# Gated attention and expert layer: the attention stage's order around the maximum, and an expert stage in which GpSimd only fetches

## The chip, the cores and the metric

The kernel runs on one core of a Trainium2 chip. A core has TensorE (PE in the profile, its weight loads PEld), VectorE (DVE), ScalarE (ACT), GpSimd (POOL) and SyncE (SP), which work through their own instruction lists and wait for each other on semaphores, and 16 DMA engines. The metric is the device time of one execution in microseconds, the median of the runs.

## The reference

128 sequences of 128 tokens and 256 channels in float32 pass through a windowed attention over a context, and then through a layer with 16 experts of which each token takes two:

```
x = x + tanh(g_xattn) * attention(layernorm(x), ctx, ctx)      # 16 heads of 16, rope, |i-j| <= 64, softmax, output projection
x = x + tanh(g_ffn) * experts(layernorm(x))
def experts(x):                          # per sequence
    probs, ei = top_k(softmax(x @ w_router), 2)
    buf[ei, pos] = x                     # 16 places for each expert and sequence, the rest is dropped
    o = (silu(buf @ w_gate) * (buf @ w_fc)) @ w_proj
    return sum(probs * o[ei, pos])
```

## The kernel before

There are three blocks, one behind the other: attention, routing, experts. Products in float32 precision are made of three passes over operands split in a head (rounded to the matmul's format) and a rest; ScalarE makes the heads ("_hi"), VectorE or GpSimd the rests ("_lo").

**Attention.** A step treats a pair of sequences; there are 64. Each engine has its list of the step's parts written out by hand (its `step(s)`), in which parts of several pairs are interleaved: at step s the scores, maxima, exponentials and values are those of pair s, the projections of keys and queries those of pair s + 1, the transposes of the input those of s + 2, the output projection that of s - 1, the second norm and the router those of s - 2. The two sequences of a pair are its halves b = 0 and b = 1. For each half TensorE writes scores in the four banks ST0 to ST3 (L680, with the band mask L685); VectorE takes partial maxima (`partial_max`, L506, one of each bank); TensorE turns them (`turn_max`, L693); VectorE makes the shift (`shift_of`, L513 and L517); TensorE subtracts it in the banks (`subtract_max`, L700); ScalarE takes the exponentials (`exp_unit`, L360); TensorE multiplies with the values (`values_unit` 0 to 3, L712, one for each bank) into the bank PO, which ScalarE copies out (`copy_out_t`). Then TensorE transposes back (`untranspose`, L724), VectorE divides (`normalise`: the reciprocal L525, the product L527), TensorE transposes the attention output (`attention_t`, L730), and ScalarE and VectorE split it (`attention_head`, at_hi, L401; `attention_rest`, at_lo, L565) for the output projection. L730 is also the line of the transposes of the input (`inputs_t`) and of the second norm (`normed2_t`). VectorE's `scale` makes q_cos and q_sin, from which GpSimd makes q_rot, and ScalarE q_head.

**Experts.** A step treats one unit, 128 in all: one sequence in the parts that move tokens, one pair of experts over a group of 8 sequences in the parts that multiply. The constants LOAD, PICK, DISPATCH, GATE, HIDDEN, OUTPUT, FETCH, COLLECT (L1047) say by how many steps a part lags: a part with lag -11 treats unit u + 11 at step u. SyncE loads a sequence's normed tokens (scaled<-xn_d), ScalarE rounds them (x_hi), GpSimd takes the rest (x_lo, L1163), VectorE builds the 0/1 matrix `pick` (L1219), TensorE gathers with it into DS (L1304), ScalarE and VectorE split the result (s_hi, s_lo). For a pair of experts TensorE multiplies (GU, L1260 to L1262), ScalarE takes tanh of half the gate (th, L1196), VectorE makes (th + 1) * gate (L1236) and the product with the other half (hid, L1240), TensorE transposes (HT) and multiplies (EO); the result goes to memory (eo_d). GpSimd fetches each token's two rows from there with two indirect DMAs (L1154, `first` and `second`), SyncE fetches the attention's result (scaled<-x_d), and VectorE adds them, weighted (L1229, L1244), which SyncE writes out. The names th, hid and scaled are tiles in SBUF; `scaled` here holds the tiles of loaded and finished tokens. The halving in silu(g) = g (1 + tanh(g / 2)) / 2 lies in `weight` (L984).

## Time and profile before

| | |
|---|---|
| median of 3 runs | 1761.66 us (1759.19 to 1764.53) |
| the profiled execution's own time | 1754.3 us |
| its span, first to last instruction | 1752.5 us |
| mean granted TensorE clock | 0.96 |
| busy over the span | PE 1481.3, DVE 1408.6, ACT 1146.4, POOL 1086.1 us |
| attention stage | about 0 to 1200 us |
| routing | about 1200 to 1264 us |
| expert stage | about 1264 to 1752 us |

The table's times are of one execution. Busy time adds up an engine's instructions; an instruction's recorded time can overlap the next one's by 0.1 us or so, so the distance between starts says what an instruction costs its engine.

### The profile page before, as it was taken

Reading aid. Unit: us, or ns where it says so; the run is one execution under the profiler, and the core shown is the slowest. Engines: PE = TensorE matmul, PEld = TensorE weight load, DVE = VectorE, ACT = ScalarE, POOL = GpSimd, SP = SyncE. Lnnn points to the kernel's source line nnn. Section 1 sums busy time; section 2 is a strip of 40 time slices with the busy share of each in tenths; the row PEclk is TensorE's granted clock in tenths of the full one; section 3 lists DMA queues with packets and bytes.
Section 4 is the critical chain, followed back from the end, with each engine's and each line's share of the span. In section 5 each row is a group of like instructions: output and inputs, shape, how many; then the busy total and the mean of one; then the engine's idle time right before and its main releaser. Section 6 shows DMA issues by size and latency. Waiting matters only on the chain. (4 is left out here: it accounts for less than half of the span.)

```text
span 1752.5 us, 50746 instructions
## 1 busy us (share of the span) xinstructions
PE 1481.3 (85%) x16844; PEld 1195.2 (68%) x16844; DVE 1408.6 (80%) x2993; ACT 1146.4 (65%) x2321; POOL 1086.1 (62%) x1490
## 2 busy tenths in 40 slices
PE   3899999999999999999999999982199888888881
PEld 3676667777776676777676677761088888888881
DVE  3788888888888888878888888867878999999984
ACT  3777777777777777777777777764065555555550
POOL 3555656565655656565565656534638887888876
PEclk9999999999999999999999999995589999999995
DMA  3122121212222121212212121430037888888887
GB/s 94 50 76 75 61 89 60 90 60 84 65 67 82 60 90 60 90 60 78 71 62 88 60 90 60 137 119 30 15 106 245 260 261 258 261 273 263 264 261 223
DMA packets 156096, 210.21 MB, mean 120 GB/s; under 512 B 18688, under 2 KB 104832, under 8 KB 156032
## 3 DMA queue, kind: packets, MB, share of 16 engines
q1 hardware_dynamic: 125312, 142.36, 25.9%
q0 software_dynamic: 12288, 33.57, 6.7%
q10 hardware_dynamic: 18432, 33.56, 5.3%
q8 instruction: 24, 0.39, 0.1%
q14 instruction: 40, 0.33, 0.1%
HBM read 125.54 MB, written 83.89 MB: 119 GB/s over the span
## 5 line engine op out<-in xcount | busy, mean ns | idle before, releaser
L506 DVE TRANSPOSE_TENSOR_REDUCE part_max<-ST 128x16 f32<-128x512 f32 x512 | 321.3, 685 | 136.6 <-PE ST L685 136.6
L360 ACT ACTIVATE probs_t<-ST 128x512 f32<-128x512 f32 x512 | 264.4, 604 | 27.6 <-PE ST L700 27.4
L712 PE MATMUL PO<-probs_t,v_aug 128*32 128x128 f32 x4096 | 193.6, 284 | 67.9 <-ACT probs_t L360 55.4
L299 POOL TENSOR_TENSOR k_rot<-k_cos,k_sin 128x256 f32<-128x256 f32 x64 | 47.1, 736 | 268.5 <-DVE k_sin L544 268.5
L712 PEld LDWEIGHTS PO<-probs_t,v_aug 128*32 128x32 f32 x4096 | 88.9, 109 | 161.1 <-ACT probs_t L360 154.0
L1191 ACT ACTIVATE x_hi<-scaled 128x256 fp32r<-128x256 f32 x128 | 53.5, 418 | 214.8 <-DMA scaled<-xn_d 168.5
L401 ACT ACTIVATE at_hi<-F 128x512 fp32r<-128x512 f32 x64 | 38.2, 597 | 187.8 <-PE F L730 187.8
L1260 PE MATMUL GU<-we_hi,s_hi 128*128 128x256 f32 x512 | 155.4, 304 | 0.2 <-DVE s_lo L1250 0.2
L1154 POOL DMA_INDIRECT second<-eo_d,collect_row x128 | 123.0, 961 | 42.2 <-issue 28.6
L1163 POOL TENSOR_TENSOR x_lo<-scaled,x_hi 128x256 fp32r<-128x256 f32 x128 | 118.4, 925 | 49.3 <-ACT x_hi L1191 47.3
L1154 POOL DMA_INDIRECT first<-eo_d,collect_row x128 | 124.4, 972 | 37.3 <-issue 20.6
L1261 PE MATMUL GU<-we_hi,s_lo 128*128 128x256 f32 x512 | 144.9, 283 | 0.0
L1262 PE MATMUL GU<-we_lo,s_hi 128*128 128x256 f32 x512 | 144.8, 283 | 0.0
L316 POOL TENSOR_TENSOR q_rest<-q_rot,q_head 128x512 f32<-128x512 f32 x64 | 82.2, 1284 | 78.7 <-ACT q_head L413 78.7
L1260 PE MATMUL EO<-we_hi,h_hi 128*128 128x256 f32 x256 | 81.6, 319 | 50.3 <-issue 43.5
L730 PE MATMUL F<-ident_sb,xn 128*128 128x128 f32 x512 | 86.2, 292 | 31.1 <-ACT xn L437 19.7
L366 ACT ACTIVATE out_t<-PO 128x512 f32<-128x512 f32 x128 | 76.7, 599 | 53.2 <-PE PO L712 53.2
L1229 DVE SCALAR_TENSOR_TENSOR scaled<-first,weight,scaled 128x256 f32<-128x256 f32 x128 | 65.5, 512 | 49.6 <-issue 18.1
L1261 PEld LDWEIGHTS GU<-we_hi,s_lo 128*128 128x128 f32 x512 | 98.3, 192 | 0.0
L1260 PEld LDWEIGHTS GU<-we_hi,s_hi 128*128 128x128 f32 x512 | 97.6, 191 | 0.4 <-issue 0.4
L1262 PEld LDWEIGHTS GU<-we_lo,s_hi 128*128 128x128 f32 x512 | 97.8, 191 | 0.0
L1260 PEld LDWEIGHTS EO<-we_hi,h_hi 128*128 128x128 f32 x256 | 48.3, 188 | 70.0 <-issue 68.1
(158 smaller groups left out, 5610.7 us busy)
## 6 DMA issues: line engine op xcount, KB each, us to landing
eo_d<-eo ACTq DMA_DIRECT2D x128, 256.0 KB
x_in_sb<-x SPq DMA_DIRECT2D x64, 256.0 KB, 2.8
c_in_sb<-ctx_t SPq DMA_DIRECT2D x64, 256.0 KB, 2.9
xr_sb<-x SPq DMA_DIRECT2D x64, 256.0 KB, 4.0
x_d<-x SPq DMA_DIRECT2D x64, 256.0 KB, 4.0
xn_d<-xn SPq DMA_DIRECT2D x64, 256.0 KB, 4.2
scaled<-xn_d SPq DMA_DIRECT2D x128, 128.0 KB, 4.0
scaled<-x_d SPq DMA_DIRECT2D x128, 128.0 KB
```

The source lines that it names most:

```text
L316: pool.tensor_tensor(q_rest[:].rearrange("p k t -> p (k t)"), q_rot[:].rearrange("p k t -> p (k t)"), q_head[:].rearrange("p k t -> p (k t ...
L360: act.activation(probs_t[:, b, i].rearrange("p j q -> p (j q)"), ST[i][:], ACT.Exp) \
L366: act.activation(out_t[:, b].rearrange("p i q -> p (i q)"), PO[:], ACT.Copy).then_inc(M["ot_copied"], 1)
L506: dve.tensor_reduce(part_max[:, i, 0], ST[i][:].rearrange("p (c l) -> p c l", l=32), AX_X, ALU.max, apply_transpose=True).then_inc(M["part ...
L712: last = pe.matmul(PO[32 * j:32 * j + 32, i * SEQ:(i + 1) * SEQ], v_aug[:, n.par, b, head], probs_t[:, b, i, j], start=True, stop=True)
L730: last = pe.transpose(F[:, (2 * k + b) * SEQ:(2 * k + b + 1) * SEQ], src[:, b, k * P:(k + 1) * P], ident[:])
L1154: pool.indirect_dma_start(out=dst[:, n.turn(3)], out_offset=None, in_=D["eo_d"][n.group].rearrange("r e c -> (r e) c"), in_offset=bass.Ind ...
L1163: pool.tensor_tensor(x_lo[:, n.slot(2)], x_in_sb[:, n.turn(3)], x_hi[:, n.slot(2)].bitcast(F32), ALU.subtract).then_inc(M["x_lo_done"], 1)
L1229: dve.scalar_tensor_tensor(out=y_sb[:, n.slot(2)], in0=first[:, n.turn(3)], scalar=weight[:, 0, bass.ds(n.n, 1)], in1=xr[:, n.turn(3)], op ...
L1260: pe.matmul(out, lh, rh, start=first, stop=False)
L1261: pe.matmul(out, ll, rh, start=False, stop=False)
L1262: return pe.matmul(out, lh, rl, start=False, stop=last)
```

## The change

In the attention stage TensorE turns the maximum of half 0 behind three of the query projection's twelve matmuls, not six, and that of half 1 ahead of both output projections, not between them; it subtracts the shift ahead of the transposes of the attention output, not behind; the transposes of the second norm stand behind values unit 2, not ahead of it. VectorE takes the product of `normalise` behind the shift (the reciprocal stays ahead), and one of the two statistics of the norm behind the shift of half 1. ScalarE takes exponentials 0 and 1 of half 0 ahead of at_hi, and ct_hi (`context_head`) behind the exponentials of half 1.

In the expert stage x_lo is made by VectorE; GpSimd only fetches. ScalarE takes Silu in place of tanh, and VectorE's operation (th + 1) * gate is gone, with the factor 0.5 in `weight`. Rings and lags change: four tiles for loads and four for the attention's result, in which the output is now added up in place, a HEAD part of its own for x_hi, loads 14 steps ahead instead of 13, fetch and collect one step later. The lists of SyncE, ScalarE and VectorE are in another order.

```diff
@@ ACT, attention, step @@
                 normed2(s - 2)
+            if s.real:
+                exp_unit(s, 0, 0)
+                exp_unit(s, 0, 1)
             if (s - 1).real:
                 attention_head(s - 1)
             if s.real:
-                for i in range(4):
-                    exp_unit(s, 0, i)
+                exp_unit(s, 0, 2)
+                exp_unit(s, 0, 3)
                 copy_out_t(s, 0)
...
-            if (s + 2).real:
-                context_head(s + 2)
             if s.real:
                 for i in range(4):
                     exp_unit(s, 1, i)
             if (s + 2).real:
+                context_head(s + 2)
                 input_head(s + 2)
@@ DVE, attention @@
+        def reciprocals(n, b):
+            dve.wait_ge(M["o2_done"], n.n * 2 + b + 1)
+            wait_for(dve, M["att_done"], n.n * 2 + b - 1)
+            o2 = F2[:].rearrange("p (h d) -> p h d", d=32)
+            dve.reciprocal(rden[:, b], o2[:, :, DK]).then_inc(M["rden_done"], 1)
...
             if (s - 1).real:
+                reciprocals(s - 1, 1)
+            if s.real:
+                shift_of(s, 0)
+            if (s - 1).real:
                 normalise(s - 1, 1)
-            if s.real:
-                shift_of(s, 0)
...
             if s.real:
                 shift_of(s, 1)
+            if (s + 3).real:
+                norm_rest(s + 3)
@@ PE, attention, step @@
                 key_projection(s + 1)
-                query_projection(s + 1, 0)
+                query_projection(s + 1, 0, [0])
             if s.real:
                 turn_max(s, 0)
             if (s + 1).real:
+                query_projection(s + 1, 0, [1])
                 query_projection(s + 1, 1)
+            if s.real:
+                subtract_max(s, 0)
             if (s - 1).real:
                 attention_t(s - 1)
             if s.real:
-                subtract_max(s, 0)
                 values_unit(s, 0, 0)
                 values_unit(s, 0, 1)
+                values_unit(s, 0, 2)
             if (s - 2).real:
                 normed2_t(s - 2)
             if s.real:
-                values_unit(s, 0, 2)
                 values_unit(s, 0, 3)
                 scores(s, 1)
...
+            if s.real:
+                turn_max(s, 1)
             if (s - 1).real:
                 output_projection(s - 1, 0)
-            if s.real:
-                turn_max(s, 1)
-            if (s - 1).real:
                 output_projection(s - 1, 1)
@@ experts @@
-    LOAD, PICK, DISPATCH, GATE, HIDDEN, OUTPUT, FETCH, COLLECT = -13, -11, -9, 0, 2, 3, 12, 14
+    LOAD, HEAD, PICK, DISPATCH, GATE, HIDDEN, OUTPUT, FETCH, COLLECT = -14, -11, -10, -9, 0, 2, 3, 13, 15
...
-            n = unit(PICK)
-            if on(PICK):
-                pool.wait_ge(M["x_hi_done"], n.n + 1)
-                wait_for(pool, M["ds_done"], n.n - 1)
-                pool.tensor_tensor(x_lo[:, n.slot(2)], x_in_sb[:, n.turn(3)], x_hi[:, n.slot(2)].bitcast(F32),
-                                   ALU.subtract).then_inc(M["x_lo_done"], 1)
...
-                act.activation(th[:, n.slot(2)], GU[n.slot(2)][:].rearrange("p (e f n) -> p e f n", e=2, f=2)[:, :, 0],
-                               ACT.Tanh, scale=0.5).then_inc(M["th_done"], 1)
+                wait_for(act, M["ht_done"], n.n - 1)
+                act.activation(gate[:, n.slot(2)], GU[n.slot(2)][:].rearrange("p (e f n) -> p e f n", e=2, f=2)[:, :, 0],
+                               ACT.Silu).then_inc(M["gate_done"], 1)
```

TensorE's list near the end of the attention stage, where it is written out step by step; the rows begin with the last matmul of the query projection (F<-xt_lo,w_hi) of a half 0 and end with its last values unit. Before:

```order
L668 MATMUL F<-xt_lo,w_hi 128x256
L730 MATMUL F<-ident_sb,att 128x128 x4
L700 MATMUL ST<-shift,ones_r 128x512 x4
L712 MATMUL PO<-probs_t,v_aug 32x128 x8
L730 MATMUL F<-ident_sb,xn 128x128 x4
L712 MATMUL PO<-probs_t,v_aug 32x128 x8
```

and of the change:

```order
L680 MATMUL F<-xt_lo,w_hi 128x256
L712 MATMUL ST<-shift,ones_r 128x512 x4
L742 MATMUL F<-ident_sb,att 128x128 x4
L724 MATMUL PO<-probs_t,v_aug 32x128 x12
L742 MATMUL F<-ident_sb,xn 128x128 x4
L724 MATMUL PO<-probs_t,v_aug 32x128 x4
```

The subtraction has moved ahead of the attention transposes, and one values unit (four matmuls) ahead of the transposes of the second norm.

ScalarE's list at the same place, from the second norm to the copy of the transposed second norm. Before:

```order
L445 ACTIVATE xn<-x,off,rstd 128x256 x2
L401 ACTIVATE at_hi<-F 128x512
L360 ACTIVATE probs_t<-ST 128x512 x4
L366 ACTIVATE out_t<-PO 128x512
L384 ACTIVATE x2t<-F 128x512
```

and of the change:

```order
L445 ACTIVATE xn<-x,off,rstd 128x256 x2
L360 ACTIVATE probs_t<-ST 128x512 x2
L401 ACTIVATE at_hi<-F 128x512
L360 ACTIVATE probs_t<-ST 128x512 x2
L366 ACTIVATE out_t<-PO 128x512
L384 ACTIVATE x2t<-F 128x512
```

at_hi has moved between the second and the third exponential.

VectorE's list of one expert step in the middle of the stage. Before:

```order
L1214 TENSOR_TENSOR h_lo<-HT,h_hi 128x256
L1219 TENSOR_TENSOR pick<-logits,iota_sb 128x256
L1229 SCALAR_TENSOR_TENSOR scaled<-first,weight,scaled 128x256
L1236 SCALAR_TENSOR_TENSOR th<-th,GU 128x256
L1240 TENSOR_TENSOR hid<-th,GU 128x256
L1244 SCALAR_TENSOR_TENSOR scaled<-second,weight,scaled 128x256
L1250 TENSOR_TENSOR s_lo<-DS,s_hi 128x32x16
```

and of the change:

```order
L1220 TENSOR_TENSOR h_lo<-HT,h_hi 128x256
L1226 TENSOR_TENSOR x_lo<-scaled,x_hi 128x256
L1228 TENSOR_TENSOR pick<-logits,iota_sb 128x256
L1237 TENSOR_TENSOR gate<-gate,GU 128x256
L1242 SCALAR_TENSOR_TENSOR scaled<-first,weight,scaled 128x256
L1248 TENSOR_TENSOR s_lo<-DS,s_hi 128x32x16
L1253 SCALAR_TENSOR_TENSOR scaled<-second,weight,scaled 128x256
```

x_lo has come in, the operation on th is gone, and both weightings stand behind the gate's product, the second one last.

## Rows read from the trace of the kernel before

**Rows 1.** Timeline of PE, one attention pair: start us, us, engine, line, operation.

```profile
611.32 0.39 PE L680 MATMUL ST<-q_hi,k_hi 32*128 32x256 f32 x4 [0.19 <-issue]
...
615.40 0.27 PE L693 MATMUL PO<-ident_sb,part_max 128*128 128x128 f32 x1
...
616.79 0.51 PE L700 MATMUL ST<-shift,ones_r 32*128 32x512 f32 x4
618.07 0.92 PE L712 MATMUL PO<-probs_t,v_aug 128*32 128x128 f32 x16 [0.77 <-ACT probs_t L360]
618.92 0.66 PE L730 MATMUL F<-ident_sb,xn 128*128 128x128 f32 x4
619.50 0.64 PE L712 MATMUL PO<-probs_t,v_aug 128*32 128x128 f32 x16
620.08 0.39 PE L680 MATMUL ST<-q_hi,k_hi 32*128 32x256 f32 x4
...
624.49 0.27 PE L693 MATMUL PO<-ident_sb,part_max 128*128 128x128 f32 x1
...
625.88 0.51 PE L700 MATMUL ST<-shift,ones_r 32*128 32x512 f32 x4 [0.21 <-DVE shift L517]
...
629.15 0.39 PE L680 MATMUL ST<-q_hi,k_hi 32*128 32x256 f32 x4
```

**Rows 2.** Busy us and counts of two stretches, granted clock, DMA share, GB/s.

```profile
1290.00:1310.00 20.00, 20.00 (x168) 19.85 (x167) 14.80 (x34) 12.77 (x33) 4.43 (x6) 1.00 0.40 135
...
1330.00:1690.00 360.00, 317.06 (x2477) 299.23 (x2477) 333.27 (x722) 203.59 (x514) 297.04 (x309) 1.00 0.85 263
```

**Rows 3.** Groups of DVE from 1330 to 1690 us: busy, mean ns.

```profile
L1244 DVE SCALAR_TENSOR_TENSOR scaled<-second,weight,scaled 128x256 f32<-128x256 f32 x103 | 77.6, 753 | 0.0
```

**Rows 4.** Timeline of DVE, expert steps, the last row from the tail.

```profile
1453.08 0.48 DVE L1244 SCALAR_TENSOR_TENSOR scaled<-second,weight,scaled 128x256 f32<-128x256 f32 x1
...
1457.49 0.41 DVE L1214 TENSOR_TENSOR h_lo<-HT,h_hi 128x256 fp32r<-128x256 f32 x1
1457.83 0.41 DVE L1219 TENSOR_TENSOR pick<-logits,iota_sb 128x256 fp32r<-128x256 f32 x1
...
1458.55 0.41 DVE L1236 SCALAR_TENSOR_TENSOR th<-th,GU 128x256 f32<-128x256 f32 x1
...
1459.33 1.06 DVE L1244 SCALAR_TENSOR_TENSOR scaled<-second,weight,scaled 128x256 f32<-128x256 f32 x1
...
1460.91 0.41 DVE L1214 TENSOR_TENSOR h_lo<-HT,h_hi 128x256 fp32r<-128x256 f32 x1
...
1732.53 0.48 DVE L1244 SCALAR_TENSOR_TENSOR scaled<-second,weight,scaled 128x256 f32<-128x256 f32 x1
```

**Rows 5.** Timeline of DVE, the same attention pair.

```profile
612.57 2.51 DVE L506 TRANSPOSE_TENSOR_REDUCE part_max<-ST 128x16 f32<-128x512 f32 x4 [0.59 <-PE ST L685]
...
615.71 0.30 DVE L513 TENSOR_REDUCE PO<-PO 128x32 f32<-128x128 f32 x1
616.05 0.69 DVE L517 TENSOR_TENSOR shift<-PO,own_sb 128x512 fp32r<-128x512 f32 x1
...
621.32 2.51 DVE L506 TRANSPOSE_TENSOR_REDUCE part_max<-ST 128x16 f32<-128x512 f32 x4 [1.60 <-PE ST L685]
```

**Rows 6.** Timeline of ACT, the same attention pair.

```profile
616.86 0.60 ACT L401 ACTIVATE at_hi<-F 128x512 fp32r<-128x512 f32 x1 [3.09 <-PE F L730]
617.42 2.07 ACT L360 ACTIVATE probs_t<-ST 128x512 f32<-128x512 f32 x4
```

**Rows 7.** Timeline of POOL, the same expert step.

```profile
1459.98 1.00 POOL L1163 TENSOR_TENSOR x_lo<-scaled,x_hi 128x256 fp32r<-128x256 f32 x1
```

**Rows 8.** Timeline of POOL, the tail of the expert stage.

```profile
1732.03 0.94 POOL L1154 DMA_INDIRECT first<-eo_d,collect_row  x1 [0.30 <-issue]
```

**Rows 9.** Loads of xn_d from 1400 to 1600 us, issue to landing.

```profile
DMA to landing us min/median/max: 2.9/4.1/5.2
```

**Rows 10.** Timeline of ACT, start of the kernel.

```profile
0.74 1.28 ACT L351 ACT_TABLE_LOAD   x1 [0.74 <-PEq L1377]
```

More of the change, by code:

```diff
@@ L552, in norm_stats, with norm_rest @@
             wait_for(dve, M["ln_aggr"], n.n)
-            for b in range(2):
-                last = dve.bn_stats(stats[:, b], x_in_sb[:, n.par, b])
-            last.then_inc(M["ln_stats"], 1)
+            dve.bn_stats(stats[:, 0], x_in_sb[:, n.par, 0])
+        def norm_rest(n):
+            dve.bn_stats(stats[:, 1], x_in_sb[:, n.par, 1]).then_inc(M["ln_stats"], 1)
             dve.wait_ge(M["ln_stats"], (n + 1).n)
@@ L732, in transposes, with project @@
             return last
-        def project(F, w, hi, lo, m):
-            for k in range(KC):
+        def project(F, w, hi, lo, m, parts=range(KC)):
+            for k in parts:
                 last = split_matmul(F[:, m * 2 * SEQ:(m + 1) * 2 * SEQ],
@@ L771, in logits_t, with query_projection @@
             pe.transpose(F2[:, 256:320], lt_sb[:], ident[0:64, 0:64]).then_inc(M["lg_done"], 1)
-        def query_projection(n, m):
-            if m == 0:
+        def query_projection(n, m, parts=range(KC)):
+            if m == 0 and 0 in parts:
                 pe.wait_ge(M["xt_hi_done"], (n + 1).n)
                 pe.wait_ge(M["xt_lo_done"], (n + 1).n)
-            last = project(F0, 0, xt_hi, xt_lo, m)
+            last = project(F0, 0, xt_hi, xt_lo, m, parts)
             if m == KC - 1:
@@ L1183, in step @@
             if on(OUTPUT):
+                act.wait_ge(M["eo_done"], n.n + 1)
+                wait_for(act, eo_out[n.turn(3)], (n - 3).landed(3))
+                act.activation(flat(eo[:, n.turn(3)]), EO[n.slot(2)][:], ACT.Copy).then_inc(M["eo_copied"], 1)
+            n = unit(OUTPUT)
+            if on(OUTPUT):
                 act.wait_ge(M["eo_copied"], n.n + 1)
@@ L1251, in step @@
                                   tokens(s_hi, n).bitcast(F32), ALU.subtract).then_inc(M["s_lo_done"], 1)
+            n = unit(COLLECT)
+            if on(COLLECT):
+                dve.wait_ge(M["y_part_done"], n.n + 1)
+                dve.scalar_tensor_tensor(out=xr[:, n.turn(4)], in0=second[:, n.turn(3)],
+                                         scalar=weight[:, 1, bass.ds(n.n, 1)], in1=xr[:, n.turn(4)],
+                                         op0=ALU.mult, op1=ALU.add).then_inc(M["out_done"], 1)
         run_flat(dve, step)
```

107 lines of the change are left out of this document (46 added, 61 removed).

## The prediction, on record before the change ran

> **What bounds the kernel now.** I read the work of each engine by stretches first, then the timelines of one attention pair and of one expert step. The attention stage takes 64 pairs; from one pair's first scores to the next pair's is 629.15 - 611.32 = 17.83 us [rows 1]. TensorE sets it: its instructions follow each other with hardly a gap, and where it does wait, it waits for the exponentials (0.77 us at 618.07). I call the stretch from scores of half 0 to scores of half 1 "half 0" (620.08 - 611.32 = 8.76 us), the rest "half 1" (9.07 us). The expert stage is another matter. In its middle, 360 us hold 103 steps, 3.49 us each [rows 2, 3]; VectorE is busy 333 us of them, TensorE 317, and the DMA engines 0.85 of the time [rows 2]. In one undisturbed step VectorE runs without a gap from h_lo at 1457.49 to h_lo at 1460.91, 3.42 us [rows 4]: VectorE sets the step. The mean is 0.07 us more because some steps are held up by late transfers.
>
> **Attention, half 0.** The last of the four partial maxima ends at 612.57 + 2.51 = 615.08 [rows 5], while TensorE reaches the turn of the maximum only at 615.40 [rows 1], behind the whole first half of the query projection (six matmuls, 0.12 us apart, as 24 fill 2.86 us further on). After the change three matmuls of 0.12 us come behind the turn instead of ahead of it, so TensorE is there at about 615.05 and waits for the maxima: 615.08, 0.06 for the signal (shift ends at 616.74 and the subtraction starts at 616.79 [rows 1, 5]), 0.1 for the weight load, so the turn runs at 615.24. VectorE's own sequence from there is as before: the reduction started 0.31 after the turn and the shift ended 1.03 after the reduction started (615.71 to 616.74 [rows 5]); the attention product, now behind the shift, is out of the way. So the shift ends at 615.24 + 0.31 + 1.03 = 616.58 and the subtraction starts at 616.64 instead of 616.79, 0.15 us earlier. The first exponential starts 0.63 after it (616.79 to 617.42 [rows 1, 6]), at 617.27.
>
> ScalarE is where it is given back. Before, at_hi (the rounded copy of the transposed attention output) ran at 616.86 and was done at the moment when the first exponential could start, so it cost nothing [rows 6]. Now the order is exponential 0, 1, at_hi, exponential 2, 3. Exponentials are 0.49 apart ((2.07 - 0.60)/3, with at_hi's 0.60 as one's length), at_hi delays what is behind it by 617.42 - 616.86 = 0.56 [rows 6]. Exponential 2 so starts at 617.27 + 0.98 + 0.56 = 618.81 and its values can run 0.65 later (617.42 to 618.07), at 619.46. TensorE reaches that place at 617.27 + 0.49 + 0.65 + 0.29 = 618.70 and has nothing else to do there, since the transposes of the second norm (0.58: 618.92 to 619.50 [rows 1]), which filled this wait, now stand behind values unit 2. From 619.46: values 2 (0.29, half of 619.50 to 620.08), transposes 0.58, values 3 0.29; the scores of half 1 start at 620.62 instead of 620.08. Half 0 gets **0.54 us longer**. (The attention transposes do move into the wait for exponential 0, but a wait takes their place between values 1 and 2.)
>
> **Attention, half 1.** The maxima of half 1 are ready at 621.32 + 2.51 = 623.83 [rows 5], and the turn ran at 624.49 between the two output projections [rows 1]. Put ahead of both, it runs at 623.99 (signal and weight load as above), where TensorE is free since about 623.7 (624.49 less six matmuls): a wait of 0.2 to 0.35. The shift is then early and the wait for it, 0.21 us at 625.88 [rows 1], goes; but the projections start later by the wait. I count 0.12 us gained, between 0 and 0.2. What else moves is covered: at_lo, q_cos and q_sin are late by about 0.55 beyond the longer half 0's beginning and meet slack on ScalarE, because ct_hi, which now stands behind the four exponentials, has left 0.6 us ahead of them. xt_hi then ends some 0.3 us later and xt_lo still just ahead of the next maxima. Behind a late at_hi stand, in order, at_lo on VectorE, q_sin, q_rot on GpSimd, q_head; if their slack were gone, half 1 would grow too.
>
> Sum of the attention stage: +0.42 us a pair, 62 pairs with all their parts: **+26 us**; bounds 0.2 a pair (12 us) and 0.6 (37 us).
>
> **Expert stage, VectorE.** An undisturbed step is 3.42 us. The multiplication with (th + 1) goes (0.41 [rows 4], 0.44 with its share of a gap); x_lo comes from GpSimd and costs what pick does, 0.34 a step. The second weighting (L1244) takes 1.06 in this step and 0.48 in the one at 1453.08; over the stretch its mean is 0.753 [rows 3, 4]. What stretches it is GpSimd's x_lo: it starts at 1459.98 [rows 7], and the weighting ends 0.41 behind that, at 1460.39, wherever it began; both take two operands from SBUF. A fetch doesn't do this: in the tail, where no x_lo is left, the weighting at 1732.53 runs inside the fetch of 1732.03 and takes 0.48 [rows 4, 8]. With x_lo gone from GpSimd, 0.58 us of this step goes. 3.42 - 0.44 - 0.58 + 0.34 = 2.74 us.
>
> The Trainium skill ("SBUF — State Buffer", section "SBUF: two separate sides") describes an exclusive lock between a GpSimd operation and a VectorE operation with two SBUF inputs, and speaks against the change if a fetch counts as such an operation, since GpSimd now does nothing else and VectorE has four such operations a step. By it the 0.58 would come back at least once a step; the weighting in the tail shows no such thing.
>
> **What bounds the step then.** TensorE: before the weightings began, 168 matmuls and transposes of 24 a step filled 20 us, 2.86 us a step [rows 2]. GpSimd: two fetches, 2 x (0.95 + 0.30) = 2.5 us [rows 8]. DMA: 0.85 x 3.49 = 2.97 us of all engines a step, at 263 GB/s [rows 2], and the bytes stay the same. So the transfers become the nearest bound, and a FIFO of three queues isn't kept full: with transfers landing in 4.1 us (2.9 to 5.2) at 0.85 busy [rows 9], gathered rows and x1 have only some 5 to 6 us between their issue and the first weighting two steps later. I take 0.96 busy, 3.10 us a step; the ends are 2.97 and 3.35 (0.89 busy, near what they do now). Gain 0.39 us x 101 steps = **40 us**, ends 52 and 14. The earlier loads (four input tiles, an SP queue that no longer waits for the weighting) are what lets the transfers come that near.
>
> Smaller terms: the fetch is one step later, so the tail, in which only fetches run, has one more step: +2.5 us [rows 8]. Silu brings one more table load, 1.28 us like the one at the start [rows 10], nothing hides it wholly: +1.3. In the first ten dispatches x_lo of 0.7 us on GpSimd is out of the chain: -2. Silu itself and the rest of the routing cost nothing.
>
> Sum: +26 - 40 + 2.5 + 1.3 - 2 = -12 us. The profiled run took 1754.3 us (span 1752.5), 7.4 less than the median of the runs, 1761.7; I put the difference on the median: **1749 us**.
>
> **Rivals.**
> 1. The attention edits don't lose (at_hi fits, or TensorE's waits were worth more than I read): the stage stays or gains a little. For it: TensorE's waits for exponentials are the only real ones there. Against: ScalarE has no room between exponentials 1 and 2, by its own row. 1749 - 26 = 1723. Chance 0.18.
> 2. Slower: the expert step is held by transfers at 3.35 us, because a fetched row or x1 lands too late for the in-order VectorE, and the tiles' ring stops the loads: 1749 + 26 = 1775; it decides from 3.23 us a step on. For it: steps are held up already at 0.85 busy (mean 3.49 against 3.42). Against: each load is issued earlier relative to its user. Chance 0.16.
> 3. The attention stage loses 0.8 us a pair, since the chain at_lo, q_sin, q_rot, q_head has no slack after all: 1749 + 24 = 1773. Chance 0.06.
> 4. Fetches stretch VectorE as x_lo did: 2.74 + 0.58 = 3.32 us a step, 1749 + 22 = 1771. The row in the tail is against it. Chance 0.02.
> My forecast, attention slower by 12 to 37 and the expert stage faster by 30 to 50, has 0.53; 0.05 is left for what I don't see.
>
> **How the numbers follow.** A run can tell about 0.3% here, 5 us. Faster by more (under 1756): most of the forecast's 0.53 (0.41), rival 1, a little of the rest: 0.61. Within 0.3%: 0.19. Slower: rivals 2, 3, 4, less their mild ends: 0.20. The likeliest case alone spans about 1732 to 1764, as its two terms seldom stand at their ends together; the range takes in rival 1 and the nearer part of rival 2: 1722 to 1771.
>
> **What would show it.** In the profile after: the pair grows from 17.83 to about 18.25 us, TensorE idle 0.7 us ahead of values unit 2 waiting for probs_t, at_hi between exponentials; the turn in each half waits for part_max. In the expert stage L1244's successor takes 0.48 always, the step is 3.1, DMA busy 0.95 or so, and VectorE idles ahead of the first weighting. Wrong would be: a pair of 17.8 or less, a step over 3.25, or VectorE operations stretched beside fetches.

## The result, and the profile after

The changed kernel takes 1810.32 us (median of four runs, 1809.28 to 1811.09), the kernel before 1760.43 (four runs, 1759.05 to 1764.53): the ratio is 1.0276, 95% interval 1.0259 to 1.0293. It is slower by 50 us, where 1749 was forecast, and it lies outside the range. The profiled execution took 1811.1 us with a span of 1809.2, against 1754.3 and 1752.5 before.

Two places in the span carry nearly all of it. The turns of the maximum mark the attention stage; its first and last start, of the kernel before and of the changed one (the row of the line: ns minimum, median and maximum of one, first and last start in us):

```profile
L693 PE MATMUL PO<-ident_sb,part_max x128: 270/273/331, 39.8 to 1181.4; 128*128 128x128 f32 x128
```

```profile
L705 PE MATMUL PO<-ident_sb,part_max x128: 327/328/332, 38.4 to 1210.9; 128*128 128x128 f32 x128
```

That is 1141.6 us before and 1172.5 after, +30.9, for 63.5 pairs: 17.98 us a pair and 18.46. The expert stage should have given 40 us back. From the last matmul of TensorE's first GU unit to the last matmul of its last it went from 428 to 450 us instead, +22. Its middle (windows of the changed kernel: busy us and counts of the engines, granted clock, DMA share, GB/s), to be held against [rows 2]:

```profile
1330.00:1690.00 360.00, 304.10 (x2400) 294.04 (x2399) 275.52 (x678) 208.31 (x497) 184.39 (x186) 0.98 0.78 243
```

No engine is full any more. VectorE has fallen from 333 us to 276, and TensorE, the transfers (0.85 before, 0.78 now) and GpSimd have gaps as well. The step follows from the last matmul of GU in two units 90 steps apart (timeline of PE, changed kernel): (1706.06 - 1373.66) / 90 = 3.69 us.

```profile
1373.66 0.28 PE L1266 MATMUL GU<-we_lo,s_hi 128*128 128x256 f32 x1
...
1706.06 0.28 PE L1266 MATMUL GU<-we_lo,s_hi 128*128 128x256 f32 x1
```

VectorE's own terms came as forecast. Both weightings now take 0.48, in every step within 0.1 us (groups of VectorE, same stretch; the second answers to [rows 3], 753 ns before):

```profile
L1242 DVE SCALAR_TENSOR_TENSOR scaled<-first,weight,scaled 128x256 f32<-128x256 f32 x90 | 43.2, 480 | 0.0
L1253 DVE SCALAR_TENSOR_TENSOR scaled<-second,weight,scaled 128x256 f32<-128x256 f32 x90 | 43.0, 478 | 0.0
```

What VectorE waits for now is seen in one step (timeline of all engines, changed kernel, the rows that matter):

```profile
1500.08 1.05 POOL L1166 DMA_INDIRECT first<-eo_d,collect_row  x1 [1.39 <-DVE scaled L1253]
...
1501.43 0.95 POOL L1166 DMA_INDIRECT second<-eo_d,collect_row  x1 [0.30 <-issue]
...
1502.06 0.28 PE L1266 MATMUL GU<-we_lo,s_hi 128*128 128x256 f32 x1
...
1502.27 0.42 ACT L1197 ACTIVATE x_hi<-scaled 128x256 fp32r<-128x256 f32 x1 [0.46 <-issue]
...
1502.80 1.05 POOL L1166 DMA_INDIRECT first<-eo_d,collect_row  x1 [0.42 <-issue]
...
1504.34 0.39 ACT L1202 ACTIVATE gate<-GU 128x256 f32<-128x256 f32 x1 [1.65 <-remote]
...
1504.76 0.42 DVE L1237 TENSOR_TENSOR gate<-gate,GU 128x256 f32<-128x256 f32 x1 [1.73 <-issue]
...
1507.27 0.36 PE L1264 MATMUL EO<-we_hi,h_hi 128*128 128x256 f32 x1 [1.60 <-ACT h_hi L1181]
```

The last matmul of this GU unit starts at 1502.06. ScalarE is free at 1502.69 and has only this unit to wait for (its other condition, the transposes of HT, was met when h_hi ran at 1500.94), yet its Silu starts at 1504.34, 2.28 us behind the matmul. VectorE waits for Silu, and later TensorE itself waits 1.60 us for h_hi. TensorE meanwhile went on starting matmuls at 0.12 us each.

The trace also records when semaphores are updated, and there the lateness stands directly. In this step the update by which GU's last matmul tells that it is done comes 2.27 us behind the start of that matmul, and 0.02 us ahead of Silu. In the kernel before it comes 0.30 us behind in every one of units 20 to 109. In the changed kernel 79 of these 90 units have a recorded update; 60 of them come later than 0.5 us and 40 later than 1 us, up to 3.85 us. I call a completion that comes over 1 us late "held". Whether the result was late in the bank or only the signal, the trace can't tell, since the ends of matmuls are modelled in it.

A second measure, the start of Silu, is easier to take but counts more. It lies more than 1.5 us behind the start of its unit's last matmul in 52 of the 90 units. In 20 of the 52 Silu starts within 0.1 us of a late update; in the others ScalarE came late itself, often as a consequence, or no late update is recorded right ahead of it. The kernel before, with tanh in that place and another order on ScalarE, has 41 such units and not one late update. By the start of Silu the disturbance begins at unit 13 (1350.3 us); the fetches set in at 1344.5, and up to there the step is 2.85.

### The profile page after: what moved, and what is told of

It reads as the page before. It is cut to its first block and busy times, and to the rows that moved or that the text cites. A ratio compares the mean times of both kernels' runs of the same rounds, so it can differ in the third digit from the quotient of the medians.

```text
span 1809.2 us, 50617 instructions
## 1 busy us (share of the span) xinstructions
PE 1515.6 (84%) x16844; PEld 1197.1 (66%) x16844; DVE 1373.1 (76%) x2993; ACT 1154.1 (64%) x2322; POOL 977.7 (54%) x1362
## 5 line engine op out<-in xcount | busy, mean ns | idle before, releaser
L360 ACT ACTIVATE probs_t<-ST 128x512 f32<-128x512 f32 x512 | 272.4, 605 | 184.0 <-PE ST L712 184.0
L724 PE MATMUL PO<-probs_t,v_aug 128*32 128x128 f32 x4096 | 206.5, 285 | 62.2 <-ACT probs_t L360 46.3
L1166 POOL DMA_INDIRECT first<-eo_d,collect_row x128 | 130.6, 1020 | 226.8 <-DVE scaled L1253 125.9
L724 PEld LDWEIGHTS PO<-probs_t,v_aug 128*32 128x32 f32 x4096 | 84.9, 108 | 167.1 <-ACT probs_t L360 153.4
L288 POOL TENSOR_TENSOR ct_lo<-c_in_sb,ct_hi 128x512 fp32r<-128x512 f32 x64 | 82.4, 1288 | 85.9 <-ACT ct_hi L378 85.9
L445 ACT ACTIVATE xn<-x,off,rstd 128x256 f32<-128x256 f32 x128 | 70.2, 596 | 71.9 <-POOL off L329 71.9
L1237 DVE TENSOR_TENSOR gate<-gate,GU 128x256 f32<-128x256 f32 x128 | 53.8, 420 | 81.8 <-ACT gate L1202 45.0
L1248 DVE TENSOR_TENSOR s_lo<-DS,s_hi 128x512 fp32r<-128x512 f32 x128 | 88.1, 689 | 22.6 <-issue 14.3
```

What stands on the lines that cost most here:

```text
L288: pool.tensor_tensor(ct_lo[:].rearrange("p k b t -> p (k b t)"), c_in_sb[:, n.par].rearrange("p k b t -> p (k b t)"), ct_hi[:].rearrange(" ...
L360: act.activation(probs_t[:, b, i].rearrange("p j q -> p (j q)"), ST[i][:], ACT.Exp) \
L724: last = pe.matmul(PO[32 * j:32 * j + 32, i * SEQ:(i + 1) * SEQ], v_aug[:, n.par, b, head], probs_t[:, b, i, j], start=True, stop=True)
L1166: pool.indirect_dma_start(out=dst[:, n.turn(3)], out_offset=None, in_=D["eo_d"][n.group].rearrange("r e c -> (r e) c"), in_offset=bass.Ind ...
L1248: dve.tensor_tensor(tokens(s_lo, n), DS[n.slot(2)][:].rearrange("p (k e s) -> p (k e) s", k=KC, s=CAP), tokens(s_hi, n).bitcast(F32), ALU. ...
```

## The experiments

Each set of kernels that ran together had one chip to itself, with the kernel before beside it; the five sets had five chips (for the runs of the result above the chip isn't on record). That turned out to matter.

**First set: halves apart, and work for GpSimd.** The kernel before with the changed expert stage alone, and with the changed attention stage alone:

```diff
 # e1_expert_only: attention_block of before, expert_block of the change
-        then(dve.tensor_scalar(weight[:], prob[:], gates[:, 3:4], 0.5, ALU.mult, ALU.mult))
+        then(dve.tensor_scalar(weight[:], prob[:], gates[:, 3:4], None, ALU.mult))
 # e2_attention_only: attention_block of the change, the rest of before
```

> The kernel before with the changed expert stage alone, its attention stage as before. The profiles give the two halves as +31 us for the attention stage (a pair of 18.46 us against 17.98) and about +20 us for the expert stage (a step of 3.6 to 3.8 us against 3.49). If the halves add up, this kernel takes 1760 + 20 = 1780 us (1774 to 1787), ratio 1.011. If the expert stage is only long because the attention stage leaves something behind (buffers, code, clock), it takes 1720 to 1735 us, as the prediction had it.

> The changed attention stage alone, with the expert stage of the kernel before. If the halves add up: 1760 + 31 = 1791 us (1785 to 1796), ratio 1.017. If most of the difference between the two kernels lies in the expert stage: below 1775 us.

Measured: the expert stage alone 1693.13 us (1692.28 to 1695.11), ratio 0.9619 [0.9602, 0.9635]; the attention stage alone 1794.33 us, ratio 1.0196 [1.0178, 1.0214]. The second is +34 us, near what the profile said: its attention stage takes 1173 us, and its expert stage some 4 us more than before. The first was a surprise: 67 us faster than before, and the same code that made the changed kernel's step 3.69 us. In its middle everything is full (windows of this kernel):

```profile
1340.00:1640.00 300.00, 296.05 (x2470) 294.04 (x2469) 285.36 (x711) 209.13 (x508) 206.35 (x208) 1.00 0.96 315
```

and in a step like the one above, with this pair of fetches at the same place (the next pair starts 1.06 us behind the matmul there, 0.74 above), Silu runs right behind x_hi, 0.55 us behind its unit's last matmul, where the changed kernel had 2.28 (timeline of this kernel):

```profile
1499.91 1.05 POOL L1153 DMA_INDIRECT first<-eo_d,collect_row  x1 [0.95 <-DMA eo_d<-eo]
...
1501.27 0.95 POOL L1153 DMA_INDIRECT second<-eo_d,collect_row  x1 [0.30 <-DMA eo_d<-eo]
...
1501.88 0.28 PE L1253 MATMUL GU<-we_lo,s_hi 128*128 128x256 f32 x1
...
1502.10 0.42 ACT L1184 ACTIVATE x_hi<-scaled 128x256 fp32r<-128x256 f32 x1 [0.46 <-ACT eo L1174]
...
1502.43 0.37 ACT L1189 ACTIVATE gate<-GU 128x256 f32<-128x256 f32 x1
```

GU's update comes 0.30 us behind the last matmul in all 90 units here. The step is (1602.82 - 1341.22) / 90 = 2.91 us:

```profile
1341.22 0.28 PE L1253 MATMUL GU<-we_lo,s_hi 128*128 128x256 f32 x1
...
1602.82 0.28 PE L1253 MATMUL GU<-we_lo,s_hi 128*128 128x256 f32 x1
```

The other two gave GpSimd work between its fetches again, x_lo itself, or subtractions whose result nobody reads:

```diff
 # e3_xlo_gpsimd: x_lo moved from VectorE's list to GpSimd's, behind the fetch
+            if on(PICK):
+                pool.wait_ge(M["x_hi_done"], n.n + 1)
+                wait_for(pool, M["ds_done"], n.n - 1)
+                pool.tensor_tensor(x_lo[:, n.slot(2)], x_in_sb[:, n.turn(4)], x_hi[:, n.turn(4)].bitcast(F32),
+                                   ALU.subtract).then_inc(M["x_lo_done"], 1)
 # e4_spare_gpsimd: x_lo stays on VectorE
+                wait_for(pool, M["x_lo_done"], n.n)
+                for k in range(2):
+                    wait_for(pool, M["spare_done"], n.n * 2 + k)
+                    pool.tensor_tensor(spare[:], ident[:], ident[:], ALU.subtract).then_inc(M["spare_done"], 1)
```

> The changed kernel with x_lo computed on GpSimd again, behind its two fetches, and all else as changed. Theory A: GpSimd that does nothing but fetch issues the gathers in bursts, and in a burst TensorE's completions reach ScalarE and VectorE 1 to 3 us late; x_lo between the fetches spaces them, and the step falls from 3.7 us to 3.4 to 3.5: 1780 to 1790 us. Theory B: the new order on ScalarE and VectorE makes the step long, whoever computes x_lo: 1805 to 1820 us. Theory C: the step is held by transfers: no change, 1805 to 1815 us, with the DMA share unchanged at 0.78.

> The changed kernel with two subtractions of 128x128 on GpSimd in each expert step, whose result nobody reads, behind its two fetches; x_lo stays on VectorE. Theory A (the burst of fetches delays completions): spacing alone is enough, the step falls to 3.4 to 3.5 us and the time to 1780 to 1790 us. Theory B (the order on the other engines): 1805 to 1820 us. If it needs x_lo off VectorE as well, this one stays at 1810 while the one with x_lo on GpSimd falls.

Measured: 1797.78 us (ratio 1.0219 [1.0200, 1.0238]) and 1791.71 us (1.0191 [1.0166, 1.0216]), steps of 3.59 and 3.54 us, none with held completions. I would have read that as theory A come true, but the chip of this set held no completions in the kernel without spacing either, so they say nothing on it. What they do show is what GpSimd's list costs. In the timeline of GpSimd (e4) it hardly stops, at 3.49 us a step:

```profile
1449.17 0.96 POOL L1167 DMA_INDIRECT first<-eo_d,collect_row  x1 [0.37 <-DVE scaled L1261]
1450.44 0.94 POOL L1167 DMA_INDIRECT second<-eo_d,collect_row  x1 [0.30 <-issue]
1451.41 0.88 POOL L1178 TENSOR_TENSOR before_f<-ident 128x128 f32<-128x128 f32 x2
1452.66 0.96 POOL L1167 DMA_INDIRECT first<-eo_d,collect_row  x1 [0.37 <-DVE scaled L1261]
```

VectorE has room in that kernel: it waits for fetched rows (waits of VectorE, e4, 1390 to 1690 us: us in total, times, longest):

```profile
DVE scaled L1250 <- DMA second<-eo_d,collect_row: 46.3, 69, 2.5
```

The kernel before looks the same with x_lo in that place, 3.42 us from fetch to fetch in the step of [rows 7]:

```profile
1457.75 0.96 POOL L1154 DMA_INDIRECT first<-eo_d,collect_row  x1 [0.18 <-issue]
...
1461.17 0.97 POOL L1154 DMA_INDIRECT first<-eo_d,collect_row  x1 [0.18 <-issue]
```

So GpSimd, not VectorE alone, set the step of before. Taking work off its list is worth most of the 67 us: e4 lies 65 us above the 1760 + 34 - 67 = 1727 us to which the two halves of this set add up.

**Second set: which order in the attention stage leaves something behind.** All four have the changed expert stage. The first adds only waits that are long met, to move VectorE's code; the others take the changed order of one or two engines in the attention stage.

```diff
 # e5_dve_shift, at the head of VectorE's expert list
+        for _ in range(28):
+            dve.wait_ge(T["w_landed"], 16)
 # e6_pe_act_order: lists of TensorE and ScalarE as changed; VectorE's of before
 # e7_pe_order: TensorE's alone
 # e9_dve_order: VectorE's alone
```

> The kernel with the changed expert stage alone (1693 us), with 28 waits that are long met, which build into 14 instructions, ahead of VectorE's expert code: the number by which the changed attention stage makes VectorE's code longer. Nothing else differs. Theory D (the place of VectorE's code decides whether TensorE's completions are held in the expert stage): the held completions appear, the step is 3.6 to 3.8 us, 1770 to 1785 us. Theory E (the order of the attention stage itself decides): no effect, 1690 to 1697 us.

> The changed expert stage with the attention stage's changed orders on TensorE and ScalarE, VectorE's as before. The attention stage's +31 us is in TensorE's half 0 (a late turn, then late exponentials): then 1693 + 25 to 31 = 1718 to 1724 us with an undisturbed expert stage. Theory D: VectorE's code is where it was, so the expert stage is undisturbed. Theory E: if TensorE's or ScalarE's order brings the held completions, 1800 to 1810 us.

> As the one before with TensorE's order alone. By the prediction's terms the turn behind a projection half is what costs: 1693 + 20 to 31 = 1713 to 1724 us. If the late at_hi on ScalarE is what costs, under 1705 us. With held completions in the expert stage: 80 us more.

> As the one before with VectorE's order alone (reciprocal ahead of the shift, statistics in two parts). In the attention stage it should cost nothing or gain 2 to 5 us: 1688 to 1697 us. Theory D: VectorE's code has moved by 14 instructions, so the completions are held and it takes 1770 to 1785 us.

Measured: 1695.44, 1732.43, 1844.68 and 1792.38 us. Not one has held completions: the expert stage takes 362 to 366 us in all four, with steps of 2.89 to 2.92. I took theory D as fallen, but it is the fourth set that rules it out: this chip held none whatever the code, so these runs say nothing on D or E.

The attention stage differs widely. By the turns' first and last start it takes 1180 us with TensorE's and ScalarE's orders, 1296 with TensorE's alone, 1243 with VectorE's alone; all three together had 1172, none 1142. Three of these expectations missed: TensorE's and ScalarE's orders cost 38 us and not 25 to 31, TensorE's alone 154 and not 20 to 31, and VectorE's alone 101 where I expected nothing. TensorE's timelines (e9 first, then e7) show what it waits for in each pair:

```profile
647.31 0.66 PE L740 MATMUL F<-ident_sb,att 128*128 128x128 f32 x4 [0.74 <-DVE att L531]
```

```profile
652.57 1.63 PE L712 MATMUL PO<-probs_t,v_aug 128*32 128x128 f32 x24 [1.18 <-ACT probs_t L360]
```

With VectorE's order alone the attention product comes behind the shift while TensorE still wants it ahead of the subtraction; with TensorE's alone the exponentials wait for at_hi, whose transposes now come late. The rest is the clock. Once the stage is under way (from the seventh pair on, turn to turn of half 0), a pair takes 18.84 us on average in e9 where the granted clock stays at 1.00, against 17.94 before, and 20.4 in the 27 of 57 pairs that hold a stretch at 0.50. In e7 all 57 pairs hold one.

**Third set: the changed kernel again.** Unchanged, with VectorE's code moved, and with two attention edits taken back:

```diff
 # e11_after_dve_shift: the 28 waits, as in e5
 # e12_at_hi_first, ScalarE; e13_at_hi_norm2 has it too
             if (s - 1).real:
                 attention_head(s - 1)
             if s.real:
                 exp_unit(s, 0, 0)
                 exp_unit(s, 0, 1)
                 exp_unit(s, 0, 2)
                 exp_unit(s, 0, 3)
 # e13_at_hi_norm2, TensorE
-                values_unit(s, 0, 2)
             if (s - 2).real:
                 normed2_t(s - 2)
             if s.real:
+                values_unit(s, 0, 2)
                 values_unit(s, 0, 3)
```

> The changed kernel unchanged, beside the three below on one chip. If the long expert steps (3.69 us in steps 20 to 110, where the same expert code behind the attention stage of before, or behind three mixed orders of it, takes 2.89 to 2.92) belong to the program, 1808 to 1812 us again. If they belong to the chip or the day, 1720 to 1730 us: the attention stage's 31 us and an expert stage of 364 us.

> The changed kernel with 28 waits that are long met (14 instructions) ahead of VectorE's expert code. Theory F (the held completions hang on a chance of placement or phase that any small shift ends): 1722 to 1730 us, step 2.90. Theory E (the orders of the changed attention stage together leave a state behind): 1805 to 1815 us.

> The changed kernel with at_hi on ScalarE ahead of the four exponentials of half 0 again; all else as changed. By the prediction's steps at_hi between exponentials 1 and 2 is what makes half 0 longer. With it ahead, the first exponential waits for at_hi instead, if the attention transposes, which now stand behind the subtraction, come too late for it: they start 0.5 us behind the subtraction's start, take 0.66, and at_hi 0.6: the first exponential starts 1.2 us later than it could. So the stage between the first and the last turn gets longer than 1172 us, 1180 to 1230, if the transposes decide, and shorter, 1150 to 1165, if only at_hi's place did. The expert stage is 364 us or 450 us by the two theories of the other runs.

> As the one before, and the transposes of the second norm stand ahead of values unit 2 again, where they can fill a wait for the exponentials. Against the kernel with at_hi alone moved back, 0.3 to 0.58 us a pair less (19 to 36 us over the stage), if TensorE waits there; none if it doesn't.

Measured: 1817.84 (ratio 1.0304 [1.0282, 1.0326]), 1814.35, 1912.58 and 1840.91 us. All four have held completions from unit 13 on and steps of 3.68 to 3.77. The attention stage takes 1267 us with at_hi first and 1200 with the transposes of the second norm moved back as well: at_hi ahead of the exponentials costs 94 us more than at_hi between them, so the place that I blamed in the prediction is the better one, once the attention transposes stand behind the subtraction. Both expectations missed, 1267 us against 1180 to 1230, and 67 us less against 19 to 36. Most of each miss is clock: at full clock a pair takes 19.01 us in e12, 18.73 in e13 and 18.46 in the changed kernel, and of 57 pairs 38 hold a stretch at 0.50 in e12, 7 in e13 and none in the changed kernel.

**Fourth set: program or chip, and attention edits singly.** Two kernels with the changed expert stage and a part of the attention edits, then the expert-only kernel and the changed kernel unchanged.

```diff
 # e14_trio: TensorE subtracts ahead of attention_t; ScalarE at_hi behind exponentials 0 and 1;
 # VectorE, with reciprocals() of the change:
             if (s - 1).real:
-                normalise(s - 1, 1)
+                reciprocals(s - 1, 1)
             if s.real:
                 shift_of(s, 0)
+            if (s - 1).real:
+                normalise(s - 1, 1)
 # e15_turn, TensorE
-                query_projection(s + 1, 0)
+                query_projection(s + 1, 0, [0])
             if s.real:
                 turn_max(s, 0)
             if (s + 1).real:
+                query_projection(s + 1, 0, [1])
                 query_projection(s + 1, 1)
```

> The changed expert stage (1693 us behind the attention stage of before) with three of the attention edits, which belong together: the subtraction ahead of the attention transposes, the attention product behind the shift, at_hi behind exponentials 0 and 1. The transposes of the second norm stay ahead of values unit 2 and the turns where they were. By the prediction's steps at_hi then delays exponential 2 by 0.56 us, but the transposes (0.58) fill that wait: between the first and last turn 1142 to 1155 us. If these three alone bring most of the changed stage's 31 us: 1160 to 1172 us. Expert stage, last TensorE step against first: 364 us if the chip or the whole of the changed attention stage holds the completions, 450 if these three do.

> The same with one attention edit: the turn of half 0's maximum between the halves of the query projection's first half. By the prediction the shift comes 0.15 us earlier, behind a wait for the maxima of 0.05 to 0.2 us on TensorE: between the first and last turn 1135 to 1145 us. If TensorE's wait for the maxima is longer than read, up to 1155. Expert stage 364 us, or 450 if this chip holds the completions.

> The changed expert stage behind the attention stage of before once more, now on the same chip as the changed kernel below. If the program decides whether completions are held: 1692 to 1697 us again, expert steps of 2.90. If the chip decides (the runs without held completions and those with them had different chips): the same on both kernels of this call, either 1693 and 1725, or about 1780 and 1810.

> The changed kernel on the same chip as the three above. If the program decides: 1808 to 1818 us with expert steps of 3.7. If the chip decides: it goes with the kernel above, 1725 if that one takes 1693, 1810 if it takes 1780.

Measured: 1883.88, 1780.96, 1779.70 and 1806.65 us. The expert-only kernel, 1693 us in the first set, takes 1779.70 here (ratio 1.0084 [1.0066, 1.0103]), with held completions and a step of 3.68 (its middle):

```profile
1340.00:1640.00 300.00, 254.46 (x1966) 246.23 (x1965) 231.41 (x574) 172.90 (x410) 162.85 (x165) 0.96 0.81 251
```

So it is not the attention stage that makes the difference, and not the program, which is the same line for line: it goes with the chip, or with the hour, or with whatever else differed between two sets, which this can't tell apart. Theories B, D and E fall with it, as causes by themselves. The kernel before took 1760.44, 1757.84, 1763.84 and 1765.09 us in the four sets; it hardly notices. In the third set's kernels and here held completions appear in all eight, in the first two sets in none of the eight, seven of which have the changed expert stage.

The turn alone costs little: the stage takes 1148 us, +0.10 us a pair. The three edits together take 1249 us, far more than the 1142 to 1155 that the prediction's steps gave. The reason stands in TensorE's timeline (e14, half 0 from the subtraction on):

```profile
652.87 0.50 PE L710 MATMUL ST<-shift,ones_r 32*128 32x512 f32 x4 [0.41 <-DVE shift L520]
653.30 0.66 PE L740 MATMUL F<-ident_sb,att 128*128 128x128 f32 x4
654.14 0.91 PE L722 MATMUL PO<-probs_t,v_aug 128*32 128x128 f32 x16 [0.19 <-ACT probs_t L360]
655.94 0.63 PE L740 MATMUL F<-ident_sb,xn 128*128 128x128 f32 x4 [0.88 <-DVE at_lo L572]
```

The transposes of the second norm write the same F as the attention transposes and must wait until at_lo has read it. With at_hi between the exponentials at_lo is late, and TensorE stands 0.88 us, in every pair. Behind values unit 2, where the change has them, they don't wait. And the wait can have a second price (windows of e14: 3.4 us right behind such a wait, then a stretch around the next such wait, the one at 655.94, and the whole stage):

```profile
635.90:639.30 3.40, 3.40 (x46) 2.42 (x46) 0.84 (x2) 1.56 (x4) 1.42 (x2) 0.50 0.00 0
655.00:658.00 3.00, 2.12 (x50) 1.59 (x46) 1.89 (x3) 1.76 (x5) 1.77 (x4) 1.00 0.02 9
...
100.00:1150.00 1050.00, 939.06 (x11419) 703.09 (x11423) 773.30 (x1699) 726.39 (x1380) 563.48 (x904) 0.95 0.20 66
```

In the first of these the granted clock is 0.50, the lower of the two levels (1.2 GHz); in the second it stays at 1.00 behind the same wait. The 27 of 57 pairs without a stretch at 0.50 take 18.2 to 19.1 us in this kernel (18.85 on average, against 17.94 before), the 30 with one 20.2 to 20.6. So of the 107 us that the stage grows by, some 57 are waits and some 46 the clock. The kernels of before, of the change, and with the turn alone have 1.00 over the stage, though TensorE stands 0.77 us in each pair of before [rows 1].

**Fifth set: spacing.** The expert-only kernel with one subtraction on GpSimd in each step, and without.

```diff
 # e18_one_spare, GpSimd's list, behind the two fetches
+            n = unit(PICK)
+            if on(PICK):
+                wait_for(pool, M["x_lo_done"], n.n)
+                wait_for(pool, M["spare_done"], n.n)
+                pool.tensor_tensor(spare[:], ident[:], ident[:], ALU.subtract).then_inc(M["spare_done"], 1)
```

> The changed expert stage behind the attention stage of before (1693 us on two chips, 1780 on a third), with one subtraction of 128x128 on GpSimd in each step whose result nobody reads, behind the two fetches. It makes GpSimd's step 2.2 + 0.45 + 0.4 = 3.05 us at least: some 15 to 20 us over the undisturbed stage, 1708 to 1715 us, on a chip that doesn't hold completions. On one that does: theory A (fetch pairs that follow each other within 0.4 us hold them, and work between the pairs ends that) gives the same 1708 to 1715 us, against 1780 for the kernel below; theory G (the load on the DMA engines as such holds them) gives 1765 to 1790 us for both.

> The same without the subtraction, on the same chip: 1692 to 1697 us where completions are not held, 1776 to 1782 where they are. It tells which kind of chip this call has; if it is 1693, the kernel above says only what the spacing costs.

Measured: 1714.18 us (ratio 0.9738 [0.9719, 0.9756]) and 1693.09 us (0.9615 [0.9593, 0.9636]). This chip doesn't hold completions, so the question for which the pair was made is open: it shows only that the spacing costs 21 us (a step of 3.12 us), and that 1693 comes again on another chip.

## Why the prediction was wrong, point by point

**VectorE's step: right.** 2.74 us was forecast. In the changed kernel, from h_lo to h_lo without a gap (timeline of VectorE), it is 1501.94 - 1499.22 = 2.72:

```profile
1499.22 0.42 DVE L1220 TENSOR_TENSOR h_lo<-HT,h_hi 128x256 fp32r<-128x256 f32 x1
...
1501.94 0.42 DVE L1220 TENSOR_TENSOR h_lo<-HT,h_hi 128x256 fp32r<-128x256 f32 x1
```

The weighting was stretched by GpSimd's x_lo and not by a fetch; rival 4 is out. The exclusive lock of the Trainium skill ("SBUF — State Buffer", section "SBUF: two separate sides") doesn't catch a fetch here, by the mean of 478 ns.

**What bounds the step then: wrong, and this is the step that failed.** The prediction put the transfers next, 3.10 us a step, a gain of 40 us. That term of its sum, -40 us, came out as +22 in the changed kernel, and this makes the difference between 1749 and 1810. Where nothing disturbs it the step is 2.89 to 2.92 us: below even the lower bound of 2.97, since that was 0.85 x 3.49, and the same bytes kept the engines busy for only 0.96 x 2.91 = 2.79 us when the queues were full. TensorE, at 2.85, is the bound there, and the gain is 67 us. On the chips of the third and fourth set, and in the run that counts, the step was 3.68 to 3.77 us. Neither the forecast nor rival 2 (3.35) had that, and rival 2's mechanism was not it: the DMA share fell to 0.78, and VectorE's first weighting waited for no row. The loss came with completions of TensorE that reach the others up to 3.85 us behind the start of the last matmul, where 0.30 is usual. The profile of before holds no instance of it, so no row could have priced it.

**Who set the step before: half read.** I named VectorE, 3.42 us without a gap. GpSimd was equally full: two fetches of 0.95 with up to 0.30 behind each and x_lo of 1.00 [rows 7, 8] are 3.4 to 3.5 us, and e4 shows that such a list holds the step at 3.49 while VectorE has room. The sum wasn't hurt, since the change relieves both.

**Attention, half 0: right.** Forecast 9.30 us from scores to scores. Timeline of TensorE, changed kernel, against [rows 1]:

```profile
624.94 0.39 PE L692 MATMUL ST<-q_hi,k_hi 32*128 32x256 f32 x4 [0.19 <-issue]
...
628.76 0.33 PE L705 MATMUL PO<-ident_sb,part_max 128*128 128x128 f32 x1
630.21 0.51 PE L712 MATMUL ST<-shift,ones_r 32*128 32x512 f32 x4
630.64 0.66 PE L742 MATMUL F<-ident_sb,att 128*128 128x128 f32 x4
631.48 0.91 PE L724 MATMUL PO<-probs_t,v_aug 128*32 128x128 f32 x16 [0.18 <-ACT probs_t L360]
632.95 0.42 PE L724 MATMUL PO<-probs_t,v_aug 128*32 128x128 f32 x8 [0.55 <-ACT probs_t L360]
633.30 0.66 PE L742 MATMUL F<-ident_sb,xn 128*128 128x128 f32 x4
633.89 0.43 PE L724 MATMUL PO<-probs_t,v_aug 128*32 128x128 f32 x8
634.25 0.39 PE L692 MATMUL ST<-q_hi,k_hi 32*128 32x256 f32 x4
```

It is 9.31 us. The subtraction comes 5.27 us behind the scores, 5.47 before; from there to the scores of half 1 it takes 4.04 against 3.29. The wait ahead of values unit 2 is 0.55 (0.7 forecast), and at_hi stands between the exponentials (timeline of ScalarE), as forecast:

```profile
630.83 1.08 ACT L360 ACTIVATE probs_t<-ST 128x512 f32<-128x512 f32 x2 [2.08 <-PE ST L712]
631.80 0.60 ACT L401 ACTIVATE at_hi<-F 128x512 fp32r<-128x512 f32 x1
632.28 1.11 ACT L360 ACTIVATE probs_t<-ST 128x512 f32<-128x512 f32 x2
```

**Attention, half 1: a small miss.** A gain of 0.12 was forecast. The next half 1 takes 643.28 - 634.25 = 9.03 us, 0.04 less than in [rows 1], and the one ahead of it 9.33 (pairs alternate by 0.26 us, as they did before), since the turn's wait for the maxima is 0.41 and not 0.2 to 0.35 (0.41 stands in the row of its weight load). On the average of the stage's middle half 0 grew by 0.55 us and half 1 shrank by 0.04. A pair costs +0.49 us on average over the stage where 0.42 was forecast, the stage +31 where 26 was; rival 1 and rival 3 are out.

**The transposes of the second norm and at_hi: read wrongly.** The prediction said that these transposes filled the wait for the exponentials and lost that use by their move. Where at_hi stands between the exponentials they can't fill it: e14 shows that there they wait for at_lo. Nor is at_hi's place a blunder of its own, by e12. The loss seems to belong to the whole move of the attention transposes behind the subtraction: it puts at_hi, and all that depends on it, behind the first exponentials or ahead of them on a ScalarE that has no room for it. That is argued and not shown, since no run takes back the subtraction's move by itself.

**Small terms.** From the last turn to the first GU the kernel takes 1 us more, and behind the last GU 4.3 us more (45.1 against 40.8), 5 in all where 2.5 + 1.3 - 2 was forecast; behind the last GU it is 2.7 in the expert-only kernel.

The 1727 us that the halves add up to, inside the range forecast, are a sum for a chip without held completions and not a run: the changed kernel ran in three sets, and each time they were held. Had it been measured, it would have been near the forecast partly by luck, with a gain of 67 us in the expert stage where the bound that the prediction named allowed at most 52.

What holds completions is not settled. The suspicion that pairs of fetches within 0.4 us of each other do it is not shown: by the recorded updates, groups of late completions begin anywhere from 0 to 2.8 us behind the start of a fetch of first rows, and on three chips the same bursts of fetches held nothing. Load on the DMA engines alone (theory G) has something against it: the kernel before keeps them busy 0.85 of the time, more than the changed kernel's 0.78, and took 1765.09 us on the chip where the expert-only kernel took 1779.70, some 7 us above its shortest of the five sets where the other is 87 above its own. But its step of 3.49 us also leaves room to hide a delay. Whether work between the pairs would end the held completions where they occur wasn't reached, nor whether they belong to a chip for good.

The version that beats both is the attention stage of before with the changed expert stage: 1693 us in the first and fifth set (1695 in the second, with the added waits), 0.96 of before. On the chip of the fourth set it was 1780, 0.8% slower than before.

## What to carry to other kernels

Once the engine that sets a step is relieved, the next bound comes from the list of all engines that are nearly full, GpSimd's issues included, and a kernel that runs at every limit at once can lose over a fifth of a stage on one chip and nothing on another: time such a version on more than one chip before its halves are compared. An experiment on a chip that doesn't show the effect says nothing on its cause. An order is a property of several engines together: all three lists cost 31 us together, VectorE's alone 101 and TensorE's alone 154 (ScalarE's alone wasn't run), so take a coupled edit back whole. Where TensorE is almost never idle, a wait costs its own length and, in some pairs, the clock behind it.

## What the runs showed of the hardware

- Completions of TensorE can reach the waiting engines late while the matmuls go on starting at 0.12 us each: of GU's last matmuls in 90 units of the changed kernel, 79 have a recorded update, and 40 of these come over 1 us behind the start, up to 3.85 us (up to 5.7 in e12). In the expert-only kernel of the first set all 90 come within 0.30 us; the same code in the fourth set has late ones. There the step is 3.68 us, 0.77 more than in the first set.
- In a stage that is otherwise full, a pause of 0.88 us on TensorE in each pair was followed at once by a stretch at 0.50 granted clock in 30 of 57 pairs (e14), and the stage's mean clock was 0.95. The length of one pause doesn't decide it: with 1.2 us for the exponentials in each pair, 57 of 57 pairs hold such a stretch in e7 (mean 0.92), 38 in e12 (0.94) and 7 in e13 (0.99), and the kernel before, with 0.77 us in each pair, has none. The changed kernel, whose longest pause there is 0.55 us, kept 1.00.
- The same bytes kept the DMA engines busy for 2.97 us a step at 0.85 and for 2.79 at 0.96 share: a share times a step is no lower bound for the step.
